# Post-LN decoder layer: VectorE turns the cross-attention's x1 in 32x32 blocks, and the masking constant moves to PSUM

## The reference

```python
x = _layernorm(x + _L0_attn_ref(x, w_qkv, w_out))      # FFT token mixing, cumulative sum over tokens
x = _layernorm(x + _L0_xattn_ref(x, ctx, ctx, mask, W_q, b_q, ...))
x = _layernorm(x + _L0_ffn_ref(x, kernel, bias, a, b)) # one linear layer, weight quantised to int4, plus low rank
```

```python
q = _split_heads(queries @ W_q + b_q); k = ...; v = ...
scores = jnp.einsum('bhqd,bhkd->bhqk', q, k) / jnp.sqrt(jnp.float32(d))
scores = jnp.where(mask == 0, jnp.float32(-1000000.0), scores)
out = jnp.einsum('bhqk,bhkd->bhqd', jax.nn.softmax(scores, axis=-1), v)
```

## Time and profile before

| | |
|---|---|
| median of 3 runs | 943.35 us (940.66 to 944.55) |
| profiled execution | 941.81 us, of which the span on the core is 939.4 us |
| PE busy over the span | 885.9 us (94%) |
| DVE busy over the span | 669.9 us (71%) |
| ACT and POOL busy | 369.5 us (39%) and 373.9 us (40%) |
| mean granted TensorE clock | 0.975 |

### The profile page before, as it was taken

How to read it: one execution, slowest core, us unless ns; L and a number is a source line. 1 busy time by engine, 2 the same in 40 slices (tenths; PEclk the granted TensorE clock), 3 DMA queues, 4 the chain that set the end, 5 groups by cost and what they waited for, 6 DMA issues and landing times.

```text
span 939.4 us, 14604 instructions
## 1 busy us (share of the span) xinstructions
PE 885.9 (94%) x4284; PEld 733.5 (78%) x4284; DVE 669.9 (71%) x1132; ACT 369.5 (39%) x1403; POOL 373.9 (40%) x338
## 2 busy tenths in 40 slices
PE   5798999999999999999689999999999999999887
PEld 4683887888888888888578887888888888888675
DVE  3364467666666657567667978889788897988957
ACT  4152221212121111111487556665556655566611
POOL 2000364434353443315337544345343454434523
PEclk9897999999999999999789999999999999999999
DMA  6971710322314020104513140321403213030021
GB/s 184 283 203 48 177 45 34 102 66 70 95 39 134 22 68 23 67 24 143 180 23 101 30 136 11 97 67 32 132 11 94 67 44 119 12 93 19 18 79 45
DMA packets 85962, 76.02 MB, mean 81 GB/s; under 512 B 39895, under 2 KB 58583, under 8 KB 85919
## 3 DMA queue, kind: packets, MB, share of 16 engines
q1 hardware_dynamic: 85919, 75.49, 27.3%
HBM read 52.60 MB, written 22.87 MB: 80 GB/s over the span
## 4 chain that ended last, share of the span: by engine, by line
PE 37%; DVE 6%; ACT 5%; issue 2%; DVEq 0%; POOLq 0%; POOL 0%; ACTq 0%
PE shared_ps L130 28%; ACT probs L1410 4%; PE shared_ps L1204 3%; PE score_ps L130 3%; DVE score_ps L1715 2%; PE shared_ps L1166 1%; PE shared_ps L1237 1%; DVE top_s L1720 1%; ACT xT_hi L1423 1%; DVE xT_lo L1681 1%; DVE xT_lo L1673 1%; ACT qT_hi L1398 1%; DVE x_and_res L1761 0%; DVE pT_lo L1700 0%; DVE y L1739 0%
## 5 line engine op out<-in xcount | busy, mean ns | idle before, releaser
L1410 ACT ACTIVATE probs<-score_ps,top_s 128x77 f32<-128x77 f32 x512 | 158.8, 356 | 37.9 <-DVE top_s L1720 37.9
L1410 ACT ACTIVATION_READ_ACCUMULATOR probs<-score_ps,top_s 128x1 f32 x512 | 122.3, 239 | 0.0
L1559 POOL TENSOR_TENSOR probs<-probs,per_total 128x616 f32<-128x616 f32 x64 | 82.2, 1300 | 63.9 <-DVE per_total L1727 63.8
L1552 POOL TENSOR_TENSOR rstd<-ve,half_power 128x1 f32<-128x1 f32 x64 | 41.7, 652 | 153.4 <-DVE ve L1750 153.3
L1715 DVE COPY_PREDICATED score_ps<-hidden,masked 128x616 f32<-128x616 int32 x64 | 68.3, 1068 | 10.8 <-PE score_ps L130 10.5
L100 POOL TENSOR_TENSOR xT_lo<-x_tok,xT_hi 128x512 fp32r<-128x512 f32 x28 | 38.0, 1360 | 88.0 <-ACT xT_hi L96 88.0
L729 ACT ACTIVATE qT_hi<-vals 128x512 fp32r<-128x512 f32 x32 | 19.3, 628 | 119.1 <-POOL vals L776 103.8
L776 POOL TENSOR_TENSOR vals<-qs_prod 128x512 f32<-128x512 f32 x32 | 40.9, 1291 | 62.7 <-DVE qs_prod L862 62.7
L1417 ACT ACTIVATE pT_hi<-shared_ps 128x512 fp32r<-128x512 f32 (+1 forms) x96 | 47.7, 541 | 41.9 <-PE shared_ps L1204 41.6
L722 ACT ACTIVATE v_sb<-v_ps 128x512 f32<-128x512 f32 x32 | 18.9, 594 | 106.8 <-PE v_ps L130 106.8
L761 POOL TENSOR_TENSOR mix_rstd<-mix_ve,half_power 128x1 f32<-128x1 f32 x32 | 21.9, 686 | 94.3 <-DVE mix_ve L881 94.3
(11 more groups left out here) (210 smaller groups left out, 2641.4 us busy)
## 6 DMA issues: line engine op xcount, KB each, us to landing
x_tok<-in_x SPq DMA_DIRECT2D x32, 256.0 KB, 4.6
x_res<-in_x SPq DMA_DIRECT2D x8, 1024.0 KB, 7.3
x_between<-mix_x SPq DMA_DIRECT2D x32, 256.0 KB, 2.0
x<-x_between SPq DMA_DIRECT2D x8, 1024.0 KB, 5.6
x_tok<-x_between SPq DMA_DIRECT2D x8, 1024.0 KB, 5.7
out<-y_out SPq DMA_DIRECT2D x32, 256.0 KB, 2.0
wqkv_sb<-in_w_qkv SPq DMA_DIRECT2D x16, 192.0 KB, 5.6
keys_split<-w_q_hi SPq DMA_DIRECT2D x8, 154.0 KB, 5.3
```

What stands on the lines that cost most here:

```text
L1410: nc.scalar.activation(probs[:, t % 2, j * KEYS:(j + 1) * KEYS], score_ps[:, g, k * KEYS:(k + 1) * KEYS], ACT.Exp, bias=top[:, t % 2, j:j ...
L1552: nc.gpsimd.tensor_tensor(rstd[:, n:n + 1], ve[:, n:n + 1], half_power[:], ALU.pow).then_inc(rstd_ready, 1)
L1559: nc.gpsimd.tensor_tensor(p, p, per_total[:, t % 2, h * heads:(h + 1) * heads].unsqueeze(2) .to_broadcast([P, heads, KEYS]), ALU.mult).the ...
```

## The change

VectorE takes over the transposes of x1. The load comes in four quarters, VectorE turns four block columns in place (`turn_x1`, placed in the first half of its step), ScalarE makes the high parts from SBUF, GpSimd the low parts of columns 0 and 1, VectorE those of columns 2 and 3. Columns 0 and 1 have tiles of their own (`x1T_first`), columns 2 and 3 stay in `oT` and wait for `project_o` 3. The four uses X0 to X3 leave the bank order, and TensorE's transposes of x1 go away in every stage. W_q is loaded by 16 DMAs in interleaved rows. The constant `masked` moves to unused columns of the score banks in PSUM, once for each half of the heads. Other lines only pass slices instead of tiles.

```diff
+def load_quarters(sp, tile, src, loaded):
+    for q, part in enumerate(by_quarter(src)):
+        sp.dma_start(quarters(tile)[q * BLOCK:(q + 1) * BLOCK, :, :], part).then_inc(loaded, 16)
...
+def low_of_column(engine, hi, lo, tile, j, lo_ready, count=1):
+    engine.tensor_tensor(blocks(lo), block_column(tile, j), blocks(hi).bitcast(F32), ALU.subtract).then_inc(lo_ready, count)
...
-            sp.dma_start(x1_next[:], w_q_dram.rearrange("(c p) n -> p c n", p=P)).then_inc(wq_loaded, 16)
+            for c in range(NC):
+                load_interleaved(sp, x1_next, w_q_dram, c, wq_loaded)
...
-                if half == 0:
-                    pe.wait_ge(x1_loaded, 16)
-
-                    pe.wait_ge(kv_done, nth(B - 1, 8, 7))
-                    pe.wait_ge(qs_done, nth(B - 1, 8, 7))
-                    for c in range(NC):
-                        for t in range(NT):
-                            last = nc.tensor.transpose(next_banks[c][:, t * P:(t + 1) * P],
-                                                       x1_next[:, t, c * P:(c + 1) * P], ident[:])
-                        last.then_inc(hand.filled, 1)
-
...
             steps(dve, step)
+            dve.wait_ge(x1_loaded, 16 * NC)
+            for c in range(NC):
+                turn_block_column(nc, x1_next, c, hand.x1_turned)
             for c in range(NC):
                 dve.wait_ge(hand.x1T_hi, c + 1)
-                nc.vector.tensor_tensor(x1T[1][:, c, :], next_banks[c][:], x1T[0][:, c, :].bitcast(F32),
-                                        ALU.subtract).then_inc(hand.freed, 1)
+                low_of_column(nc.vector, *column(x1T, c), x1_next, c, hand.x1T_lo[c // 2], 2)
...
-        x1T = oT
+        x1T_first = pair("x1T_first", [P, NC // 2, S])
+        x1T = [[(first if c < NC // 2 else o)[:, c, :] for c in range(NC)] for first, o in zip(x1T_first, oT)]
...
+        masked = [score_ps[:, 2 * h, GK + 12:GK + 12 + KEYS] for h in range(2)]
...
             def load_x1(i):
 
                 wait_reuse(sp, x1T_hi, i * NC)
-                sp.dma_start(x1[:], x1_dram[i].rearrange("(t p) d -> p t d", p=P)).then_inc(x1_loaded, 16)
+                for lo in x1T_lo:
+                    wait_reuse(sp, lo, i * NC)
+                load_quarters(sp, x1, x1_dram[i], x1_loaded)
...
@@ TensorE, project_q and step
-                    pe.wait_ge(freed, s.emptied("X3"))
+                    for lo in x1T_lo:
+                        pe.wait_ge(lo, nth(i, NC, NC - 1))
...
-                turn_x1(i + 1, s, 0)
-                turn_x1(i + 1, s, 1)
-                turn_x1(i + 1, s, 2)
                 project_f(i, s, 1)
-                turn_x1(i + 1, s, 3)
...
@@ GpSimd, step
                 root(i, s, "O2")
+                split_x1(i + 1, s, 0)
                 bias_x2(i, s, 2)
                 root(i, s, "F0")
+                split_x1(i + 1, s, 1)
                 root(i, s, "O3")
                 bias_x2(i, s, 3)
...
@@ VectorE, softmax_top and step
-                                          masked[:].unsqueeze(1).unsqueeze(1).to_broadcast(shape)).then_inc(hid, 1)
+                                          masked[h].unsqueeze(1).unsqueeze(1).to_broadcast(shape)).then_inc(hid, 1)
...
                 split_probs(i, s, 0, 0)
+                turn_x1(i + 1, 0)
                 add_o(i, s, 1)
...
                 split_probs(i, s, 0, 1)
+                turn_x1(i + 1, 1)
                 invert_totals(i, 1)
...
                 split_x2(i, s, 0)
                 measure(i, s, "O2")
+                turn_x1(i + 1, 2)
                 split_probs(i, s, 0, 2)
+                turn_x1(i + 1, 3)
                 softmax_top(i, 2, 0)
...
                 softmax_top(i, 2, 1)
-                split_x1(i + 1, s, 0)
                 measure(i, s, "O3")
-                split_x1(i + 1, s, 1)
                 split_x1(i + 1, s, 2)
                 normalize_o(i, s, 3)
                 add_f(i, s, 1)
                 invert_totals(i, 2)
                 split_x1(i + 1, s, 3)
...
@@ VectorE, batch 0
             softmax_top(0, 2, 1)
+            for c in range(NC):
+                turn_x1(1, c)
             split_probs(0, s, 0, 0)
```

More of the change, by code:

```diff
@@ L462, in _ @@
                     dve.wait_ge(hand.x_hi, m - TURN_AT - 1)
-                    low_of_column(nc.vector, hand.xT[0], x_first, m - TURN_AT - 2, hand.x_lo)
+                    low_of_column(nc.vector, *column(hand.xT[0], m - TURN_AT - 2), x_first, m - TURN_AT - 2, hand.x_lo)
                 if m == 0:
@@ L508, in __init__ @@
         self.filled, self.freed = sem("shared_filled"), sem("shared_freed")
-        self.x1T_hi, self.q_hi = sem("x1T_hi_ready"), sem("q_hi_ready")
+        self.x1_turned, self.x1T_hi = sem("x1_turned"), sem("x1T_hi_ready")
+        self.x1T_lo = [sem(f"x1T_lo_ready{n}") for n in range(2)]
+        self.q_hi = sem("q_hi_ready")
 def load_keys(sp, k_dram, hand, i):
@@ L582, in load_x @@
                     sp.wait_ge(x_lo, nth(i - 2, NC, NC - 1))
-                for q, src in enumerate(by_quarter(x[i])):
-                    sp.dma_start(quarters(x_tok[half])[q * BLOCK:(q + 1) * BLOCK, :, :], src).then_inc(x_loaded[half], 16)
+                load_quarters(sp, x_tok[half], x[i], x_loaded[half])
             def load_residual(i):
@@ L715, in split_x @@
                     wait_reuse(act, q_filled, (i - 1) * 4)
-                high_of_column(nc, xT[half], x_tok[half], c, x_hi)
+                high_of_column(nc, xT[half][0][:, c, :], x_tok[half], c, x_hi)
             def copy_v(i, p, h):
@@ L747, in _ @@
             for c in range(NC):
+                act.wait_ge(hand.x1_turned, c + 1)
+                high_of_column(nc, x1T[0][:, c, :], x1_next, c, hand.x1T_hi)
+            for c in range(NC):
                 act.wait_ge(hand.filled, c + 1)
-                nc.scalar.activation(x1T[0][:, c, :], next_banks[c][:], ACT.Copy).then_inc(hand.x1T_hi, 1)
-            for c in range(NC):
-                act.wait_ge(hand.filled, NC + c + 1)
                 nc.scalar.activation(qT[0][:, c, :], next_banks[c][:], ACT.Identity,
@@ L767, in split_x @@
                 pool.wait_ge(x_hi, nth(i, NC, c))
-                low_of_column(nc.gpsimd, xT[half], x_tok[half], c, x_lo)
+                low_of_column(nc.gpsimd, *column(xT[half], c), x_tok[half], c, x_lo)
             def sum_vals(i, p, h):
@@ L1159, in _ @@
         def _(pe):
-            def turn_x1(i, s, c):
-                if c == 0:
-                    pe.wait_ge(x1_loaded, nth(i, 1, 0) * 16)
-                use = f"X{c}"
-                wait_reuse(pe, freed, s.reusable(use))
-                for t in range(NT):
-                    last = nc.tensor.transpose(shared_ps[s.bank(use)][:, t * P:(t + 1) * P],
-                                               x1[:, t, c * P:(c + 1) * P], ident[:])
-                last.then_inc(filled, 1)
             def project_q(i, s, c):
@@ L1173, in project_q @@
                     pe.wait_ge(x1T_hi, nth(i, NC, NC - 1))
-                    pe.wait_ge(freed, s.emptied("X3"))
+                    for lo in x1T_lo:
+                        pe.wait_ge(lo, nth(i, NC, NC - 1))
                 wait_reuse(pe, freed, s.reusable(use))
-                pieces = [([w[:, k, c * P:(c + 1) * P] for w in w_q], [x[:, k, :] for x in x1T]) for k in range(NC)]
+                pieces = [([w[:, k, c * P:(c + 1) * P] for w in w_q], [x[k] for x in x1T]) for k in range(NC)]
                 split_matmuls(nc, shared_ps[s.bank(use)][:], pieces).then_inc(filled, 1)
@@ L1390, in split_x1 @@
             def split_x1(i, s, c):
-                use = f"X{c}"
-                act.wait_ge(filled, s.filled(use))
-                nc.scalar.activation(x1T[0][:, c, :], shared_ps[s.bank(use)][:], ACT.Copy).then_inc(x1T_hi, 1)
+                act.wait_ge(x1_turned, nth(i, NC, c))
+                if c == NC // 2:
+                    after_projection(act, s)
+                high_of_column(nc, x1T[0][c], x1, c, x1T_hi)
             def split_q(i, s, c):
@@ L1667, in _ @@
         def _(dve):
-            nc.vector.memset(masked[:], MASKED).then_inc(masked_set, 1)
-            dve.wait_ge(masked_set, 1)
+            for half in masked:
+                nc.vector.memset(half, MASKED).then_inc(masked_set, 1)
+            dve.wait_ge(masked_set, 2)
             def remainder(s, use, hi_ready, count, hi, lo, psum):
@@ L1673, in remainder, with turn_x1 @@
                 nc.vector.tensor_tensor(lo, psum, hi.bitcast(F32), ALU.subtract).then_inc(freed, 1)
+            def turn_x1(i, c):
+                if c == 0:
+                    dve.wait_ge(x1_loaded, nth(i, 1, 0) * 16 * NC)
+                turn_block_column(nc, x1, c, x1_turned)
             def split_x1(i, s, c):
-                remainder(s, f"X{c}", x1T_hi, nth(i, NC, c), x1T[0][:, c, :], x1T[1][:, c, :],
-                          shared_ps[s.bank(f"X{c}")][:])
+                dve.wait_ge(x1T_hi, nth(i, NC, c))
+                if c == NC // 2:
+                    after_projection(dve, s)
```

(1 more changed line is left out.)

57 lines of the change are left out of this document (31 added, 26 removed).

## The result

The changed kernel takes 953.46 us (median of 4 runs, 953.38 to 955.75), against 943.75 us (940.66 to 944.55) for the kernel before beside it: a ratio of 1.0129, interval 1.0099 to 1.0159. It is slower, by 1.3%. The profiled execution has a span of 951.7 us, 12.3 us above the one before.

A forecast was written before the change was run, and what follows sets the result against it. The prediction took VectorE and TensorE as both near the limit up to the query projection, TensorE alone behind it, VectorE in the closing step. Terms 2.2 - 2.3 + 0 - 0.4 = -0.5 us gave 942.8 us, range 930 to 953.

The forecast's parts named there:

- TensorE's savings turn into waits: Repeating step: TensorE's 1.63 us become waits at the first feed-forward matmul, last output projection and first query projection.
- rivals 3 and 4: Masking copy in PSUM gets no shorter: 953.1 us, chance 0.05; or gets longer: about 962 us, chance 0.05.
- The entry: Start of the step up to the masking copy behind the V banks: 0.30 us earlier, between 0 and 1.02.
- The closing step: Only the masking copies count there, shortened to 0.81 us each: -2.3 us, bounds -1.0 and -2.7.
- Rival 1: In the loop, VectorE's path gets short enough and TensorE keeps 1.63 us a step: 930.9 us, chance 0.30.
- Of this 0.25 is slack: Before the query projection: of the last low part's 0.61 us delay, 0.25 is absorbed, leaving +0.36 us a step.
- the collisions: VectorE beside GpSimd before the last low part: +0.37 us normalising F0, +0.28 waiting for the root of O3.
- Rival 2: GpSimd wins the collisions, at column 3's low part against the bias addition: 1.91 us a step, 952.1 us, chance 0.16.
- a few us of new waits per step cost no clock in the loop: Repeating steps: TensorE's clock stays at 1.00 (2.4 GHz) despite the new waits, so no time is lost to it.
- batch 0: Ahead of the loop: TensorE's 2.47 us bank wait goes, VectorE's four turns add 2.48: 0, within 2.5 us either way.
- the change of stage: Sixteen transposes ahead of the back projection's second half go, won only until GpSimd's last remainder: -0.4 us.
- The sum: Whole kernel: 2.2 for six steps, -2.3 closing step, 0 ahead of the loop, -0.4 stage change: -0.5 us.

The follow-up runs named there:

- const_only: The kernel before with only the masking constant moved to PSUM, TensorE still turning x1: 936.16 us, ratio 0.9956.
- early_and_lows: The changed kernel with turns at the start of VectorE's step, x1 loaded in time, and all four low parts on GpSimd: 936.00 us, ratio 0.9939.
- filled_waits: The changed kernel with transposes of a constant, whose results are unused, put into TensorE's new waits: 948.03 us, ratio 1.0086 to the kernel before.
- turns_only: The changed kernel with the masking constant back in SBUF: 960.36 us, ratio 1.0224 to the kernel before.
- quarter_transposes: The kernel before with 12 of 16 transposes left out of each repeating step, VectorE's work untouched: 940.27 us, ratio 0.9990.

## Why the prediction was wrong

**Right.** VectorE's path sets the step up to the query projection, TensorE's savings turn into waits, and three of these stand where they were forecast. All 64 copies take 0.774 to 0.805 us: rivals 3 and 4 are out. The entry gained 0.36 us (forecast 0.30). The closing step gained 2.13 us alone in const_only (forecast 2.3). Rival 1 did not come about: the low part of column 3 had to come 1.4 us earlier and came 1.25 later. Its mechanism shows in early_and_lows, where VectorE's path is shorter and 0.76 us a step is kept.

**The step that failed first: "Of this 0.25 is slack".** The prediction read the 0.25 us between the last low part and the query projection as TensorE's spare time. After the change the last low part ends at 659.65 and the projection starts at 659.89: 0.24 us again, with TensorE idle ahead of it. Counted from the step's first masking copy, the low part came 1.25 us later and the projection 1.24 us, so none of the 0.25 us served as slack. Whether some of it was spare in the kernel before is open. There the projection's weight load started 0.12 us behind the low part's end, with no wait, so the low part's signal needed no more than that:

```profile
652.75 0.19 PEld L130 LDWEIGHTS shared_ps<-xT_hi,w_q_hi 128*128 128x128 f32 x1
```

In the changed kernel it started 0.23 us behind that end, and why it starts later there, no run shows. (That row names VectorE's addition as what released it, but the addition had ended 0.93 us earlier.)

**Mis-sized: the collisions.** The forecast was +0.61 us to the last low part, and it measured +1.25. From the masking copy behind the V banks to that low part's end the path grew from 26.45 us (626.18 to 652.63) to 28.06 (631.59 to 659.65), +1.61, and the entry, from the step's first copy to that one, gave 0.36 back (10.52 to 10.16). Against the forecast's terms VectorE waited 0.54 instead of 0.28 us for the root of O3, the normalising of F0 lost 0.48 instead of 0.37, and the normalising of the second tile lost 0.28, which was not counted. These are 0.65 of the difference of 0.70 on the path; the last 0.05 is what is left of shifts both ways, the largest of them 0.19 us more ahead of the first output addition and 0.26 us less ahead of the third. Rival 2 named the wrong place: at the low part of column 3 VectorE won, and GpSimd paid; GpSimd held VectorE up at the three places just named instead. Its 952.1 us lies near the measured 953.46 by chance, since the clock and batch 0 are in the latter and not in the former, and so does rival 3's 953.1.

**Wrong: "a few us of new waits per step cost no clock in the loop".** It rested on the closing step, where TensorE kept 1.00 with 7.31 of 10 us busy. In the loop two steps of six lost 1.6 us each, and filled_waits shows that it was the waits. Why two and not the other four, behind equal waits, no run shows.

**Mis-sized: batch 0.** Forecast 0 with 2.5 us either way, measured +3.04. 1.23 us is the flags' comparison, which met GpSimd's clearing: it took 1.21 or 1.30 us in four of the fourteen traces and 2.53 or 2.62 us in ten, with the constant in either place, so it belongs to no edit. In const_only and turns_only, where it was long, batch 0 is 1.28 and 1.23 us longer than before, and in turns_only, which has the same turns, the projection ran at 0.23 us apart. The other 1.8 us is thus mostly the clock behind the wait for VectorE's low parts: eight matmuls 0.20 us longer each are 1.6, and 0.2 is not assigned.

**Not told by the traces: the change of stage.** Forecast -0.4 us, and the mark of batch 0 came 0.07 us earlier. It lies between 453.26 and 455.00 us in the three traces without this part of the change and between 452.79 and 456.51 in the eleven with it, so neither number stands out.

**The sum.** Six steps were forecast at +2.2 and came to +11.40: the slack 1.5, the collisions and copies of the path 3.8, the clock 3.2, and 0.7 spread over the rest of the steps, not traced. With batch 0 and the last stretch that is the 12.3 us.

## What to carry to other kernels

Work taken off the busiest engine pays only if the engine it waits for gets no more work ahead of the same meeting point: with fewer transposes or none a step was no shorter in quarter_transposes, where VectorE's work stayed, 1.3 to 1.5 us longer at full clock in the change, which put the turns onto VectorE's path, and 1.01 us shorter in early_and_lows (0.25 of it the constant's gain), where they went into its idle places and the low parts onto GpSimd. A gap between a producer's end and its consumer's start is not slack because the consumer works in it: TensorE computed scores through the 0.25 us in the kernel before, and the delay still passed on. Behind a wait, TensorE starts some time after VectorE's end in any case, 0.05 us at the feed-forward matmul at 638.03 us before (its low part ends at 637.98) and 0.24 us at the projection after. And a load has to be moved with the first instruction that needs it, in the prologue too.

## What was unexpected of the hardware

- Equal waits did not cost equal clock: behind 0.94 and 0.74 to 0.77 us of waiting (0.68 in the first step) the same projection ran at 2.4 GHz in four steps and at 1.2 GHz, for eight matmuls, in two. Sixteen useless transposes a step, each in a wait, and sixteen in batch 0 made the kernel 0.4% faster against the changed one (ratios 1.0086 and 1.0129).
- A comparison of 128x308 int32 on VectorE took 0.31 us alone. Beside GpSimd's two clearings of a tile, of 1.38 us each, it took 1.21 to 1.30 us or 2.53 to 2.62 us: it ended behind the first clearing, and the second one took 1.55 us, or it ended behind both.
- A predicated copy of 128x616 elements within PSUM, with the constant there too, took 0.774 to 0.805 us in all 64 places, beside GpSimd or not.
